# Recommendation tower (CIN and MLP) on one core: group 0 in two parts, W1 in four pieces, and another order of SyncE's transfers

## The reference

```python
e = stack([tbl_f[ids[:, f]] for f in range(39)], axis=1)      # X0: 512 x 39 x 16
Xi = X0 = e
for W, b in ((W0, b0), (W1, b1), (W2, b2)):                   # H = 128 outputs each
    Xi = einsum('hjk,bjd,bkd->bhd', W.reshape(H, 39, Fi), X0, Xi) + b[None, :, None]
    res.append(Xi.sum(axis=2))
h = concatenate([*res, dense_ctx], axis=1)                    # 400 features
h = maximum(h @ W_top1 + b_top1, 0)                           # 512
h = maximum(h @ W_top2 + b_top2, 0)                           # 256
y = h @ W_top3
```

## Time and profile before

| | us |
|---|---|
| median of 3 runs | 671.52 |
| lowest and highest | 669.16, 676.33 |
| the profiled execution | 672.24 |
| its span, from the first to the last instruction | 670.4 |

### The profile page before, as it was taken

One profiled execution on the slowest core, in us unless ns is written; L12 is line 12 of the kernel. 1 busy time (PEld: TensorE's weight loads), 2 busy tenths in 40 slices (PEclk: granted clock), 3 DMA queues, 4 the chain that ended last, 5 costly groups with the idle time before them and its releaser, 6 DMA issues.

```text
span 670.4 us, 12252 instructions
## 1 busy us (share of the span) xinstructions
PE 638.2 (95%) x2561; PEld 471.1 (70%) x2561; DVE 541.2 (81%) x1524; ACT 508.2 (76%) x1739; POOL 366.5 (55%) x308
## 2 busy tenths in 40 slices
PE   0699989998999999999999999999999999999998
PEld 0247767776777777777777777777777777785483
DVE  0348878897889898998888898989898989899490
ACT  2137968877787878887888878887879788897393
POOL 6888636674667657665756575757685222220000
PEclk9799989999999999999999999999999999999899
DMA  6457676766766767677676767677777666567100
GB/s 224 55 99 171 119 164 118 169 119 146 148 152 146 148 145 141 149 134 168 130 168 128 168 122 168 134 159 150 163 145 151 145 150 135 136 124 218 33 0 1
DMA packets 62136, 91.16 MB, mean 136 GB/s; under 512 B 34694, under 2 KB 38707, under 8 KB 61862
## 3 DMA queue, kind: packets, MB, share of 16 engines
q0 software_dynamic: 14192, 51.02, 42.2%
q1 hardware_dynamic: 47926, 39.95, 21.1%
HBM read 10.69 MB, written 1.28 MB: 18 GB/s over the span
## 4 chain that ended last, share of the span: by engine, by line
PE 79%; DMA 10%; POOL 4%; DVE 2%; SPq 2%; issue 2%; ACT 1%; DVEq 0%; POOLq 0%; ACTq 0%
PE t_bank L470 19%; PE t_bank L471 18%; PE t_bank L472 18%; PE x_bank L432 7%; PE small_bank L455 5%; POOL emb L354 4%; DMA rep<-emb_scratch 2%; DMA shared<-rep 2%; DMA rep<-rep 2%; PE t_bank L542 1%; PE x_bank L428 1%; PE x_bank L427 1%; PE x_bank L430 1%; DMA emb_scratch<-emb 1%; DMA prod<-in_w 1%
## 5 line engine op out<-in xcount | busy, mean ns | idle before, releaser
L626 ACT ACTIVATE prod<-t_bank,x0t 128x128 f32<-128x128 f32 x1472 | 416.5, 383 | 76.5 <-PE t_bank L472 67.7
L743 DVE SCALAR_TENSOR_TENSOR prod<-t_bank,x0t,prod 128x128 f32<-128x128 f32 x1024 | 286.6, 341 | 53.8 <-PE t_bank L472 49.9
L470 PE MATMUL t_bank<-w_hi,x_hi 128*128 128x512 f32 (+1 forms) x640 | 290.4, 454 | 0.6 <-DVE x_lo L732 0.3
L471 PE MATMUL t_bank<-w_lo,x_hi 128*128 128x512 f32 (+1 forms) x640 | 247.6, 387 | 0.0
L472 PE MATMUL t_bank<-w_hi,x_lo 128*128 128x512 f32 (+1 forms) x640 | 247.1, 386 | 0.0
L354 POOL DMA_INDIRECT emb<-in_table,idx x160 | 214.2, 1339 | 48.5 <-issue 47.6
L364 POOL TENSOR_TENSOR diag<-x0t,mask 128x320 f32<-128x320 f32 x64 | 86.4, 1350 | 189.3 <-PE small_bank L455 119.1
L470 PEld LDWEIGHTS t_bank<-w_hi,x_hi 128*128 128x128 f32 x640 | 120.8, 189 | 45.9 <-issue 17.8
L471 PEld LDWEIGHTS t_bank<-w_lo,x_hi 128*128 128x128 f32 x640 | 120.8, 189 | 38.3 <-issue 15.1
L472 PEld LDWEIGHTS t_bank<-w_hi,x_lo 128*128 128x128 f32 x640 | 120.4, 188 | 23.9
L775 DVE TENSOR_TENSOR prod<-prod 128x768 f32<-128x768 f32 (+2 forms) x192 | 114.5, 596 | 0.2
(11 more groups left out here) (86 smaller groups left out, 365.5 us busy)
## 6 DMA issues: line engine op xcount, KB each, us to landing
prod<-prod POOLq DMA_DIRECT2D x63, 768.0 KB, 7.6
shared<-rep SPq DMA_DIRECT2D x96, 234.0 KB
shared<-rep SPq DMA_DIRECT2D x48, 78.0 KB
emb<-in_table,idx POOLq DMA_INDIRECT x160
G<-in_w SPq DMA_DIRECT2D x1, 2496.0 KB
rep<-rep SPq DMA_DIRECT2D x28, 78.0 KB
rep<-emb_scratch SPq DMA_DIRECT2D x20, 78.0 KB
prod<-in_w SPq DMA_DIRECT2D x1, 1536.0 KB, 8.1
```

The source lines that it names most:

```text
L470: pe.matmul(acc, hi, w1_hi[:, cols], start=True, stop=False)
L471: pe.matmul(acc, hi, w1_lo[:, cols], start=False, stop=False)
L626: last = act.activation(prod[:, s, SLOT[c] + u, :], t_bank[c % T_BANKS][:, u * H:(u + 1) * H], ACT.Copy, scale=x0t[:, s, j:j + 1])
L743: last = dve.scalar_tensor_tensor(unit, t_bank[c % T_BANKS][:, u * H:(u + 1) * H], x0t[:, s, j:j + 1], unit, ALU.mult, ALU.add)
```

## The change

- **Group 0 in two parts** of 16 samples, or 256 columns. Part 0 is rows 0 to 623 of the group, part 1 the others. Each is gathered with 5 indirect DMAs of 126 and 124 rows (ids and starts are loaded as 2 x 63 partitions with 5 columns), stored with two DMAs, loaded back with four, and has its own firsts and seconds. The seconds have a place of their own each, in `prod`. Of part 0 ScalarE's queue issues the seconds b = 2, 4, 6. Part 0's pairs (117x256) go to `prod` and their products to PSUM bank 3. Part 1's pairs are formed by VectorE at p = 7 to 13 of group 0, multiplied by TensorE at p = 10 to 16 (117x256), and biased and split at p = 17 and 18, before tile 2.
- **W1 in four pieces** of 12, 8, 8 and 11 fields, one issued before the gathers start and three behind store 0, load 0 and store 1. They are split piece by piece; the last piece is split within tile 0. TensorE waits for a piece at chunks 0, 3, 5 and 7 of the first tile.
- **Small loads** are issued by ScalarE's queue, ahead of its other work.
- **Group 1's pairs** are formed later in group 0: p = 20, 21, 23, 25, 27, 29, 31 in place of 6, 10, ..., 30, and its transposes are at p = 20 in place of 8.
- **SyncE's loop**: the store for group g + 1 stands behind the second b = 4 of group g, the load behind b = 5, and the copies behind b = 6.
- **GpSimd** gathers group 1 right behind the two parts, and group 2 within tiles 0 and 1 of group 0 (5 and 5); of group 3 4 and 5 gathers come in tiles 2 and 3. In the loop its order is as before.

The diff, cut to what the sections here speak of:

```diff
+STORE_BEHIND, LOAD_BEHIND = 4, 5
...
+PARTS = 2
+PART_COLS = COLS // PARTS
+PART_TILES = PART_COLS // P
+PART_ROWS = GROUP_ROWS // PARTS
+PART_BEGIN = (0, -(-PART_ROWS // GATHERS))
+PART_SIZE = (PART_BEGIN[1], ROW_PARTS - PART_BEGIN[1])
...
+W1_PIECES = [(0, 12), (12, 20), (20, 28), (28, F)]
+W1_EARLY = 2
+W1_CHUNKS = (0, 3, 5, 7)
...
+PART_FORM_AT = [7 + b for b in range(BLOCKS)]
+PART_PAIR_AT = [10 + b for b in range(BLOCKS)]
+PART_X1_AT = (1, 7)
+PART_LO_AT = 18
...
+FIRST_X0T_AT = 20
+FIRST_FORM_AT = [20, 21, 23, 25, 27, 29, 31]
+FIRST_PAIR_AT = [23, 26, 27, 30, 31, 34, 35]
...
+FIRST_GATHERS = [(0, 5), (5, 10), (0, 4), (4, 9)]
...
+            def load_w1(i):
+                cols = slice(W1_PIECES[i][0] * H, W1_PIECES[i][1] * H)
+                sp.dma_start(w1_raw[:, cols], w1[:, cols]).then_inc(w1_loaded[i], 16)
+            for part in range(PARTS):
+                load_part_ids(part)
+            load_w1(0)
+            sp.dma_start(pair_a_raw, pair_a).then_inc(pair_w_loaded, 16)
+            sp.dma_start(pair_b_raw, pair_b).then_inc(pair_w_loaded, 16)
             sp.dma_start(ids_all[:, :], ids).then_inc(ids_loaded, 16)
             sp.dma_start(table_at[:, :], starts).then_inc(ids_loaded, 16)
-            sp.dma_start(pair_a_raw, pair_a).then_inc(w_loaded, 16)
-            sp.dma_start(pair_b_raw, pair_b).then_inc(w_loaded, 16)
-            sp.dma_start(w1_raw, w1).then_inc(w_loaded, 16)
...
+            def factors(g, half, then_x0=False):
+                sp.wait_ge(pair_ready, g * BLOCKS)
...
+                    if then_x0 and b == STORE_BEHIND:
+                        sp.wait_ge(x0t_mm, g)
+                        store_rows(g + 1, 1 - half)
+                    if then_x0 and b == LOAD_BEHIND:
+                        load_x0(g + 1, 1 - half, [0])
...
+                sp.wait_ge(part_gathered[part], 16 * PART_GATHERS)
...
+                if part > 0:
+                    sp.wait_ge(early_pair_ready, BLOCKS)
+                for b in range(1, BLOCKS):
+                    if part > 0 or b % 2 == 1:
+                        sp.dma_start(part_second_at(part, b), rep[b:b + PAIRS, 0, cols]).then_inc(part_second[b - 1], 16)
+            store_part(0)
+            load_w1(1)
+            load_part(0)
+            load_w1(2)
+            factors_of_part(0)
+            store_part(1)
+            load_w1(3)
+            load_part(1)
+            factors_of_part(1)
+            store_rows(1, 1)
+            load_x0(1, 1, range(0, REP_ROWS, F))
             with sp.Fori(1, GROUPS - 2, 2) as odd:
                 for g, half in ((odd, 1), (odd + 1, 0)):
-                    factors(g, half)
-                    x0_of(g + 1, 1 - half, at_once=False)
+                    factors(g, half, then_x0=True)
+                    copy_x0(g + 1, 1 - half)
             factors(GROUPS - 1, 1)
...
-            for g in range(AHEAD):
-                index(g, g)
-                for i in range(GATHERS):
-                    gather(i, g)
+            for part in range(PARTS):
+                gather_part(part)
+            pool.wait_ge(ids_loaded, 16 * 2)
+            index(1, 1)
+            for i in range(GATHERS):
+                gather(i, 1)
             pool.wait_ge(small_loaded, 16 * SMALL_LOADS)
             index(AHEAD, 0)
-            for i in range(GATHERS_EARLY):
-                gather(i, 0)
...
+                        for i in range(*FIRST_GATHERS[s]):
+                            gather(i, half if s < FIRST_INDEX_TILE else 1 - half)
...
+            def part_pair_product(b):
+                pe.wait_ge(early_pair_ready, b + 1)
+                pe.matmul(part_x1, w_sum[:, b, :], first_part_pair(b),
+                          start=b == 0, stop=b == BLOCKS - 1).then_inc(early_pair_mm, 1)
+            def last_part_pair_product(b):
                 pe.wait_ge(pair_ready, b + 1)
-                pe.matmul(x1_bank[:, :], w_sum[:, b, :], pairs_of(b),
+                pe.matmul(x1_bank[:, part_cols(1)], w_sum[:, b, :], pairs_of(b, PART_J),
                           start=b == 0, stop=b == BLOCKS - 1).then_inc(pair_mm, 1)
...
+                if first_tile and c in W1_CHUNKS:
+                    pe.wait_ge(w_split_lo, W1_CHUNKS.index(c) + 1)
...
+                        if first and p == PART_X0T_AT:
+                            pe.wait_ge(x0_loaded, 16 * X0_LOADS)
+                            pe.wait_ge(x0t_ready, PART_TILES)
+                            transpose_x0(0, range(PART_TILES, TILES_PER_GROUP))
+                        if first and p in PART_PAIR_AT:
+                            last_part_pair_product(PART_PAIR_AT.index(p))
...
-            transpose_x0(0, True)
+            pe.wait_ge(early_x0_loaded, 16 * X0_LOADS)
+            transpose_x0(0, range(PART_TILES), early_x0t_mm)
             warm_up(WARM_UP[1])
             for b in range(BLOCKS):
-                first_pair_product(b)
+                part_pair_product(b)
                 warm_up(WARM_UP[2])
             warm_up(WARM_UP[3])
-            pe.wait_ge(w_split_lo, 1)
...
+            act.wait_ge(early_x0_loaded, 16 * X0_LOADS)
+            for b in range(2, BLOCKS, 2):
+                act.dma_start(part_second_at(0, b), rep[b:b + PAIRS, 0, part_cols(0)]).then_inc(part_second[b - 1], 16)
+            for s in range(PART_TILES):
+                copy_x0t(0, s, first=True)
+            split_w1_hi(W1_EARLY)
+            part_x1_hi()
...
+                if part > 0 and b >= 2:
+                    dve.wait_ge(pair_mm, b - 1)
...
+                        if first:
+                            if p == DVE_CHUNKS[0]:
+                                split_w1_lo(W1_EARLY + 1)
+                            if p in PART_FORM_AT:
+                                form_part_pairs(1, PART_FORM_AT.index(p))
+                            if p == PART_LO_AT:
+                                split_last_part_x1_lo()
...
-                form_pairs(0, 0, b, True)
-            split_x1_lo(0, 0)
+                form_part_pairs(0, b)
+            split_w1_lo(W1_EARLY)
+            split_part_x1_lo()
```

313 lines of the change are left out of this document (219 added, 94 removed).

## The result

| on one chip, in turns | us | |
|---|---|---|
| kernel before | 670.34 | median of 4 runs, 666.17 to 676.33 |
| changed kernel | 703.95 | median of 4 runs, 702.30 to 704.45 |
| ratio | 1.0487 | 95% interval 1.0445 to 1.0529 |

The change makes the kernel 4.9% slower, where 659.3 us were forecast. The profiled execution has a span of 702.6 us, 32.2 more than before.

A forecast was written before the change was run, and what follows sets the result against it. TensorE is busy 638.2 of 670.4 us, so only its idle start and group waits can be won. From 672.24: -14.1 + 4.0 + 4.2 - 2.2 - 4.1 = -12.2, so 660.0, 659.3 against the median; range 651.5 to 668.0.

The forecast's parts named there:

- What is late next is TensorE itself, at 35.4 a group.: Steady loop: with the old wait gone, TensorE alone sets the pace, 35.4 us a group.
- The rival with a held SyncE queue: Loop: a store waiting for its gathers blocks the running group's seconds; VectorE waits in 14 groups, +58.8, 719 us; chance 0.06.
- Term 4: Group 1: its wait for group 2's pairs shrinks from 4.2 to 2.0 us with the clock's cost, -2.2 us.
- term 5: Group 3 and the loop: the sooner store leaves no wait, 39.50 becomes 35.44 us, -4.1 us.
- Term 1: The start: with group 0 halved, TensorE starts at 31.1 in place of 45.2 us, -14.1 us.
- the store follows 2.8 later: Start: part 0's store comes 2.8 us after the fifth gather starts at 10.5, so at 13.3 us.
- ScalarE issues them now: Start: the eleven small loads go to ScalarE, ahead of its first split; it has until 20.3 us.
- Terms 2 and 3: Group 0: more work for part 1's products and the last W1 piece, +4.0; waiting for group 1's pairs, +4.2 us.
- term 3: Group 0 waits for group 1's pairs, stored behind part 1's factors and beside a fold: +4.2 us, bounds 0 and +8.
- The store and most of the load lie ahead of the fold: Group 0: so the fold delays group 1's first pair block little; 53.5 us was taken between 52.3 and 56.8.
- The waits only move: Groups 0 and 1: gathers and folds set the chain; group 0 loses 7.4 us, later waits stay, 669.5 us; chance 0.17.

The follow-up runs named there:

- after_pad70: The changed kernel with 70 idle VectorE instructions ahead of VectorE's first addition, so its loop begins at instruction 208: 671.4 us, ratio 1.005.
- before_new_order: The kernel before with only SyncE's new loop order (store behind block 4, load behind block 5, copies behind block 6), group 0 undivided: 665.4 us, ratio 0.994.
- after_pad70_old_order: The changed kernel with SyncE's loop in the old order and VectorE's loop at instruction 208: 675.1 us, ratio 1.008.
- p70_fold_late: The kernel of after_pad70 with the first fold behind the five gathers of tile 1 and not ahead of them: 672.2 us, ratio 1.006.
- place 138: VectorE's loop begins at its instruction 138, as in the changed kernel; the kernel before, padded to it with 11 idle instructions: 682.8 us, ratio 1.019.
- place 180: The kernel before with 53 idle VectorE instructions ahead of VectorE's first addition, so its loop begins at instruction 180: 692.6 us, ratio 1.033.

## Why the prediction was wrong

**What is late next is TensorE itself, at 35.4 a group.** This step failed, and with it the forecast. The loop was treated as untouched but for SyncE's order, and a new wait in it stood in the sum at nothing, without a reason. VectorE's code ahead of it, 11 instructions longer, moved it to a place where each jump back fetches its head again. In the traces that is 32.3 us, as much as the whole loss: the marks from the first to the last are 492.7 us apart, in after_pad70 460.5. Without it the kernel takes 671.4 us, still 12 over the forecast, for the reasons below. The rival with a held SyncE queue (719 us) had a price of the right size but another mechanism, and the runs refute it: at a good place the kernel with its order is no slower.

**Term 4 and term 5** came out, by luck in the changed kernel. The old waits are gone: group 1 takes 35.36 us for 39.66 (-4.3, forecast -2.2), and in after_pad70 no group behind it is longer than 35.4 (forecast -4.1). Term 5's mechanism is shown with the undivided group 0: before_new_order takes 35.4 us for group 3 where the kernel before takes 39.5, and gains 4.2 us in the medians and 7.5 between the same marks of the profiles. But in the changed kernel it isn't needed, since after_pad70_old_order has no such wait with the old order. And term 4's wait is gone because group 1 began late:

```profile
80.08 3.17 SPq L359 DMA_DIRECT2D shared<-rep  x3
```

```profile
96.25 0.68 DVE L935 TENSOR_TENSOR G<-shared,rep 117x512 f32<-117x512 f32 x1
```

Group 2's firsts are issued at 80.1, so its first block could hardly be formed before 84 (4 us behind, as in the earlier trace rows; an estimate), where 81.6 were forecast. VectorE came to it at 96.3 and not at 80.4. GpSimd's index additions, on which term 4 leaned, took 0.2 us each, as forecast.

**Term 1** was -9.1 and not -14.1. The step "the store follows 2.8 later" was wrong: the store came 8.6 us after the last of the five gathers was issued. "ScalarE issues them now" had been costed at nothing. The queue on which the small loads went, q10, was new, and b1's 512-byte rows were in the gathers' way. Moving them gave 5 us back at the store. These 4.3 us are most of the 5.0 that the term was off; the halved load took 5.0 us (19.33 to 24.37) where 4.5 had been taken and a whole one takes 5.45.

**Terms 2 and 3** were +8.2 and came to +19.2. The mechanism of term 3 was named, group 1's pairs late behind a fold, and its bound of +8 was half of what came. "The store and most of the load lie ahead of the fold" was the wrong step: store at 44.4, load at 47.6, and the fold at 47.5, right on it. The load took 10.0 us where 5.5 had been read. p70_fold_late shows the fold's part in it. Not foreseen was that TensorE would stand 4.0 us at the transposes already. Of the 59.5 us from the first chunk to the end of group 0 it is idle for 10.3 and busy for 49.2, in part at the low clock; before, it was busy for 40.2 of 40.3. The sum over terms 1 to 3, -5.9 by the forecast and +10.1 in the traces, makes the divided start a loss by itself.

**The rivals.** "The waits only move" (669.5) is close to what the change gives without the fetches, 671.4, but by luck. Its reason for the start, rows that come late behind folds, is what the start's kernels show. But it kept 8.3 us of waits in groups 1 and 3 that are gone, and it had the first chunk 5 us too early and group 0 some 8 us too short.

The upper end of the range, 668.0, doesn't follow from its terms: start at 32, term 3 at +8 and term 4 at nothing give 659.3 + 0.9 + 3.8 + 2.2 = 666.2. The measured 703.95 lies outside either way.

## What to carry to other kernels

Before you put instructions ahead of a hardware loop, count where each engine's loop begins and ends; here a body of 320 instructions that came to lie 11 further on cost a fetch at each jump back, behind whatever the DMA engines were doing. The sign is a wait "<-issue" at the first instruction of the body and more packets on the instruction queue; some idle instructions ahead of the loop are a cure and a test. And a sooner start is worth only what the second group can follow: look first for what the next rows wait for and what the sooner work will throw in their way.

## What the runs showed that was not expected

- A jump back to code that had to be fetched again held VectorE for 2.4 to 3.4 us at DMA shares from 0.03 to 0.66, for 3.5 to 3.9 at 0.70 to 0.80 and for 5.6 to 6.5 at 0.91 to 0.94. Its cost to the kernel goes at place 138 from 2 us to 6 each time; TensorE went on for 4.5 us of the long ones and then stood.
- The same six waits are shorter at place 180 than at 138 and cost more, 22 us for 13. TensorE's clock is part of it (0.96 for 1.00 in the long groups); the rest is not settled.
- Four broadcasts of 64 KB in rows of 512 bytes, issued on another queue before the last gathers were out, delayed five gathers of 126 rows by 5 us.
- 768 KB of a fold beside a load of 246 KB in pieces of 64 bytes: the load takes 9.4 to 10.0 us, alone 5.3.
